# Latent attention with a gated feed-forward on one core: VectorE's remainder and low part between its two maxima, content copies in one write, numerators summed at other times

## What is computed

```python
xn  = layernorm(x)
q_c = ((xn @ Wq_down) @ Wq_up) as heads x 4;   q_r = (xn @ Wq_rope) as heads x 64
c_kv = xn @ Wkv_down;  k_c, v_c = c_kv @ Wk_up, c_kv @ Wv_up as heads x 4;  k_r = xn @ Wk_rope
a   = softmax((q_c . k_c + q_r . k_r) / sqrt(68))
s   = (a @ v_c) @ Wo
f   = lin(silu(lin(xn, w1q, a1, b1)) * lin(xn, w3q, a3, b3), w2q, a2, b2)
out = x + s * silu(f)          # lin(x, w, A, B) = x @ tile(w, 4).T + (x @ A.T @ B.T) / 2
```

## Time and profile before

| what | value |
|---|---|
| median of 3 runs | 2048.97 us (2047.34 to 2050.12) |
| profiled execution, its own time | 2049.55 us |
| its span, first to last instruction | 2046.7 us |
| mean granted TensorE clock | 0.986 of full speed |
| busy: PE, DVE, ACT, POOL | 92%, 71%, 68%, 69% of the span |
| chain that ended last: PE, DVE, DMA | 38%, 15%, 15% |

### The profile page before, as it was taken

How to read it: one execution, slowest core, us unless ns; L and a number is a source line. 1 busy time by engine, 2 the same in 40 slices (tenths; PEclk the granted TensorE clock), 3 DMA queues, 4 the chain that set the end, 5 groups by cost and what they waited for, 6 DMA issues and landing times.

```text
span 2046.7 us, 41685 instructions
## 1 busy us (share of the span) xinstructions
PE 1883.9 (92%) x12538; PEld 1479.3 (72%) x12538; DVE 1457.1 (71%) x1510; ACT 1386.3 (68%) x1884; POOL 1411.2 (69%) x1470
## 2 busy tenths in 40 slices
PE   9899999999999989998999999999999999887898
PEld 7777777777777767777777777777777777664666
DVE  8567777777776767677777777777767676565555
ACT  5557777777777777777777777777777776543222
POOL 5318787878778787878787878787877878104452
PEclk9999999999999999999999999999999999998999
DMA  8744444444444444444444444444444444555442
GB/s 262 205 92 109 92 107 91 104 96 99 102 100 91 94 104 91 108 93 110 90 106 91 105 96 99 102 100 104 93 99 90 108 92 99 138 125 162 146 134 72
DMA packets 186536, 225.23 MB, mean 110 GB/s; under 512 B 59710, under 2 KB 113758, under 8 KB 186462
## 3 DMA queue, kind: packets, MB, share of 16 engines
q1 hardware_dynamic: 186438, 224.57, 46.8%
q10 hardware_dynamic: 48, 0.03, 0.0%
HBM read 61.26 MB, written 35.65 MB: 47 GB/s over the span
## 4 chain that ended last, share of the span: by engine, by line
PE 38%; DVE 15%; DMA 15%; issue 13%; SPq 12%; POOL 2%; ACT 1%; DVEq 0%; ACTq 0%; POOLq 0%
PE st L1129 11%; DMA slot<-mrow 10%; PE pj L1163 8%; PE sx L1142 7%; DVE slot L1049 6%; PE ob L1095 6%; DVE mx L1041 6%; PE ob L1163 3%; SPq L740 2%; SPq L790 2%; DMA x_raw_h<-o_scratch 2%; SPq L736 2%; DVE kx L1035 1%; DVE pw L1063 1%; SPq L99 1%
## 5 line engine op out<-in xcount | busy, mean ns | idle before, releaser
L866 POOL TENSOR_TENSOR pw<-pf,pw 128x1024 f16<-128x1024 f32 x348 | 791.9, 2290 | 253.9 <-ACT pw L1022 214.0
L1041 DVE TENSOR_REDUCE mx<-sx 128x4 fp32r<-128x1024 f32 x512 | 627.1, 1225 | 450.0 <-PE sx L1142 445.2
L1129 PE MATMUL st<-slot,k 128*128 128x512 f32 x1024 | 418.2, 408 | 55.5 <-DMA slot<-mrow 47.0
L1013 ACT ACTIVATE pf<-st 128x1024 f32<-128x1024 f32 x464 | 446.5, 1011 | 33.0 <-PE st L1129 30.7
L1142 PEld LDWEIGHTS sx<-k,slot 88*128 88x128 f32 x2048 | 307.4, 191 | 165.6 <-DVE mx L1041 112.6
L1022 ACT ACTIVATE pw<-pf 128x1024 f16<-128x1024 f32 x348 | 355.2, 1055 | 93.0 <-PE ob L1095 82.3
L1142 PE MATMUL sx<-k,slot 88*128 88x256 f32 x2048 | 344.6, 291 | 75.5 <-DVE mx L1041 58.8
L1129 PE MATMUL st<-slot,krlh 128*128 128x512 f32 x1024 | 405.9, 396 | 0.0
L957 ACT ACTIVATE slot<-ob 64x512 fp32r<-64x512 f32 x256 | 151.6, 592 | 218.6 <-PE ob L1163 215.5
L1129 PEld LDWEIGHTS st<-slot,k 128*128 128x128 f32 x1024 | 194.3, 190 | 122.9 <-issue 82.6
L1129 PEld LDWEIGHTS st<-slot,krlh 128*128 128x128 f32 x1024 | 195.1, 191 | 36.3
(11 more groups left out here) (246 smaller groups left out, 2575.9 us busy)
## 6 DMA issues: line engine op xcount, KB each, us to landing
slot<-slot SPq DMA_DIRECT2D x256, 256.0 KB, 3.1
k<-kc SPq DMA_DIRECT2D x256, 128.0 KB
w_stage<-in_Wq_rope SPq DMA_DIRECT2D x64, 256.0 KB, 4.5
o_scratch<-o_sb SPq DMA_DIRECT2D x256, 64.0 KB
c_scratch<-stage SPq DMA_DIRECT2D x32, 256.0 KB, 3.1
c_in<-c_scratch SPq DMA_DIRECT2D x128, 64.0 KB, 2.2
k<-kc SPq DMA_DIRECT2D x128, 48.0 KB
k<-kx SPq DMA_DIRECT2D x128, 48.0 KB
```

What stands on the lines that cost most here:

```text
L866: nc.gpsimd.tensor_tensor(pw[:, s, kt, 1], pf[:, 2 * odd + kt], pw[:, s, kt, 0], ALU.subtract).then_inc(lo_done[kt][odd], 1)
L1013: nc.scalar.activation(dst, st[:, kt], ACT.Exp, scale=SCALE).then_inc(exp_done, 1)
L1041: nc.vector.tensor_reduce(mx[:, p, lo:lo + 4], sx[:, :, :].rearrange("p a (b k) -> p (a b) k", b=2), axis=AX.X, op=ALU.max).then_inc(red_d ...
L1129: last = nc.tensor.matmul(st[:, kt, h, :].rearrange("p (e n) -> p e n", e=PH), kk, q[:, s, :, h, :], start=(n == 0), stop=(n == 1))
```

## The change

1. **Content.** `content_hi` writes blocks 1 and 2 with one instruction (64 x 1024, `c_in` read twice), at s = 1 in place of s = 0. `content_lo` writes blocks 0 and 3 with one instruction (64 x 2 x 512), between the two maxima at s = 3 in place of behind both at s = 0. POOL's copies and their semaphore are gone. The blocks are now low, high, high, low, and the products that use them have the same sum.
2. **Remainder on DVE.** For one pair of steps of a turn it stands where it stood (it is now written at the start of the next step). For the other it moves from the end of an odd step to between the two maxima of the step behind it.
3. **PE.** In the two turns of the first group and of the last whose probabilities aren't split, `turn(k-8)` comes before `project(k)`.
4. **Finish.** Parts 0 to 5 of chunk 0 go to six tiles of their own and are loaded at k = 16 of the loop's last steps, parts 6 and 7 at k = 18. For the other chunks a pair of parts is loaded and added in each tile i, with the residual of that tile behind them, and the four `normalise` follow behind the loop over i. `output_hi` and `output_lo` of chunk c move from the `y` part of chunk c-1 into the tiles of chunk c itself: ACT at m = 8 and 9, DVE at m = 9 and 10. In DVE's step 18 a reciprocal comes earlier, and `b2` waits for all eight sums of chunk 0.

```diff
+def blocks_of(c):
+    return c[64:128, :].rearrange("p (i n) -> p i n", i=4)
+def twice(c_in):
+    return c_in[64:128, :].unsqueeze(1).broadcast_to([64, 2, CH])
...
-                        copies(k // NS + 1, at.turn(k) + 1)
-                        hold(pool, passed, ct_copy, 2 * at.turn(k) + 4)
...
-                nc.scalar.activation(content[parity % 2][:, 0, :], c_in[64:128, :], ACT.Copy).then_inc(ct_hi, 1)
+                nc.scalar.activation(content[parity % 2][:, 1:3, :], twice(c_in), ACT.Copy).then_inc(ct_hi, 1)
...
-                if s == (2 if at.first and k < NS else 0) and k < STEPS and at.live(k + NS):
+                if s == (2 if at.first and k < NS else 1) and k < STEPS and at.live(k + NS):
                     content_hi(k // NS + 1, at.turn(k) + 1)
...
-                nc.vector.tensor_tensor(c[:, 2, :], c_in[64:128, :], c[:, 0, :], ALU.subtract).then_inc(ct_lo, 1)
+                nc.vector.tensor_tensor(c[:, 0:4:3, :], twice(c_in), c[:, 1:3, :], ALU.subtract).then_inc(ct_lo, 1)
...
             def body(at, k):
+                split = k % 2 == 0 and at.live(k - 5) and at.split(k - 5)
+                if split and k % NS == 0:
+                    remainder(at, k - 5)
...
-                    for half in range(2):
-                        maxima(at, k - 1, half)
-                if k % NS == (2 if at.first and k < NS else 0) and k < STEPS and at.live(k + NS):
-                    content_lo(k // NS + 1, at.turn(k) + 1)
-                if k % 2 and at.live(k - 4) and at.split(k - 4):
-                    dve.wait_ge(hi_done[1][1], at.pairs(k - 4))
-                    nc.vector.tensor_tensor(pw[:, k % NS, 1, 1], pf[:, 3], pw[:, k % NS, 1, 0],
-                                            ALU.subtract).then_inc(lo_done[1][1], 1)
+                    maxima(at, k - 1, 0)
+                    if split and k % NS == 2:
+                        remainder(at, k - 5)
+                    if k % NS == 3 and k < STEPS and at.live(k + 1):
+                        content_lo(k // NS + 1, at.turn(k) + 1)
+                    maxima(at, k - 1, 1)
...
+                if k % NS == 0 and at.live(k - 2 * NS) and not at.split(k - 2 * NS):
+                    turn(at, k - 2 * NS)
                 project(at, k)
...
             load_num(sp, 0)
+            for n in range(KD + 2):
+                load_num_part(sp, 0, n)
...
+                if c + 1 < NC and i + 1 < NI:
+                    for n in range(2 * i + 2, 2 * i + 4):
+                        load_num_part(sp, c + 1, n)
...
-            if c + 1 < NC:
-                summed(c + 1)
             for i in range(NI):
                 if c + 1 < NC:
-                    normalise(c + 1, i)
+                    for n in (2 * i, 2 * i + 1):
+                        summed(c + 1, n)
...
+            if c + 1 < NC:
+                for kt in range(KD):
+                    normalise(c + 1, kt)
...
+                if m in (8, 9):
+                    for kt in (0, 1) if m == 8 else (2, 3):
+                        output_hi(c, kt)
...
+            dve.wait_ge(num_done, 2 * KD)
             nc.vector.scalar_tensor_tensor(out=blocks(b2), in0=blocks(hh[:, 0, :]), scalar=mk[:, 7:8], in1=b2_raw,
...
-                if starting(c) and m in (3, 4):
-                    for kt in (0, 1) if m == 3 else (2, 3):
-                        output_lo(0, kt)
+                if m in (9, 10):
+                    for kt in (0, 1) if m == 9 else (2, 3):
+                        output_lo(c, kt)
...
-                if c + 1 < NC:
-                    output_lo(c + 1, i)
```

More of the change, by code:

```diff
@@ L451, in scalar @@
                     act.wait_ge(c_loaded, 32)
-                    nc.scalar.activation(kc[64:128, 0:CH], c_in[64:128, :], ACT.Copy).then_inc(ct_hi, 1)
+                    nc.scalar.activation(blocks_of(kc)[:, 1:3, :], twice(c_in), ACT.Copy).then_inc(ct_hi, 1)
         def vector(dve):
@@ L548, in vector @@
                     dve.wait_ge(ct_hi, 1)
[L549 removed]
+                    nc.vector.tensor_tensor(blocks_of(kc)[:, 0:4:3, :], twice(c_in), blocks_of(kc)[:, 1:3, :],
                                             ALU.subtract).then_inc(ct_lo, 1)
@@ L646, in attention @@
         vt = sb(ctx, "vt", [128, 3, 4 * PH * NS * HD], BF16)
-        content = [c[64:128, :].rearrange("p (i n) -> p i n", i=4) for c in (kc, kx)]
+        content = [blocks_of(c) for c in (kc, kx)]
         krh = kc[0:64, :]
@@ L746, in content_split @@
             hold(sp, passed, ct_lo, at.turn(k) + 1)
-            hold(sp, passed, ct_copy, 2 * at.turn(k) + 2)
         def first_content(sp):
@@ L838, in body @@
                         pool.wait_ge(k1_filled, k + 3)
-                    if s == 2 and at.live(k + 2):
-                        if at.live(k - NS):
-                            hold(pool, passed, st_done, 2 * u - 6)
-                        if at.live(k - 5):
-                            if at.split(k - 5):
-                                hold(pool, passed, lo_done[0][1], at.pairs(k - 5))
-                            else:
-                                hold(pool, passed, vx_ready, u - 4)
-                        if k == 14 and not at.last:
-                            hold(pool, passed, w_ready, NS * at.g + NS + 1)
-                        copies(k // NS + 1, at.turn(k) + 1)
-                        hold(pool, passed, ct_copy, 2 * at.turn(k) + 4)
                 if at.live(k - 4) and k - 4 < STEPS:
@@ L907, in planes @@
                             ins.then_inc(vx_ready, 2)
-            def copies(parity, t):
-                c = content[parity % 2]
-                hold(pool, passed, ct_hi, t + 1)
-                for i in (1, 3):
-                    nc.gpsimd.tensor_copy(c[:, i, :], c[:, 0, :]).then_inc(ct_copy, 1)
             def refill(g, s):
@@ L1034, in content_lo, with remainder @@
                 dve.wait_ge(ct_hi, t + 1)
-                nc.vector.tensor_tensor(c[:, 2, :], c_in[64:128, :], c[:, 0, :], ALU.subtract).then_inc(ct_lo, 1)
+                nc.vector.tensor_tensor(c[:, 0:4:3, :], twice(c_in), c[:, 1:3, :], ALU.subtract).then_inc(ct_lo, 1)
+            def remainder(at, k):
+                dve.wait_ge(hi_done[1][1], at.pairs(k))
+                nc.vector.tensor_tensor(pw[:, k % NS, 1, 1], pf[:, 3], pw[:, k % NS, 1, 0],
+                                        ALU.subtract).then_inc(lo_done[1][1], 1)
             def maxima(at, k, half):
@@ L1157, in project @@
                 for c in range(KD):
-                    if c == 2 and k % NS == 0 and at.live(k - 2 * NS):
+                    if c == 2 and k % NS == 0 and at.live(k - 2 * NS) and at.split(k - 2 * NS):
                         turn(at, k - 2 * NS)
@@ L1304, in finish @@
     num_done = sem("num_done")
-    part_loaded = [sem(f"part_loaded{i}") for i in range(4)]
+    part_loaded = [sem(f"part_loaded{i}") for i in range(KD + 3)]
     xt_loaded = [sem(f"xt_loaded{i}") for i in range(2)]
@@ L1443, in sync_tail @@
             load_den(sp, 1)
+        if k == 18:
+            sp.wait_ge(num_done, KD)
             sp.wait_ge(r_stored, 16)
             spread_den(sp, 0)
-        if k == 18:
+            for n in range(KD + 2, 2 * KD):
+                load_num_part(sp, 0, n)
+        if k == 19:
             sp.wait_ge(recip, 2)
             store_recip(sp, 1)
-        if k == 19:
-            sp.wait_ge(at_sems.st_done, 2 * NS * NT)
-            for n in range(2 * KD):
-                load_num_part(sp, 0, n)
     def sync_rest(sp):
@@ L1469, in chunk @@
                 load_num(sp, c + 1)
-                for n in range(2 * KD):
+                for n in range(2):
                     load_num_part(sp, c + 1, n)
@@ L1514, in pool_rest, with summed @@
     def pool_rest(pool):
-        def summed(c):
-            pool.wait_ge(num_loaded, (c + 1) * 16 * KD)
-            for n in range(2 * KD):
-                if n >= KD:
-                    pool.wait_ge(num_done, c * 2 * KD + n - KD + 1)
-                pool.wait_ge(*parts_landed(c, n))
-                nc.gpsimd.tensor_tensor(num[:, n % KD, :], num[:, n % KD, :], num_part(c, n)[0],
-                                        ALU.add).then_inc(num_done, 1)
+        def summed(c, n):
+            tile, loaded, earlier = num_part(c, n)
+            if n == 0:
+                pool.wait_ge(num_loaded, (c + 1) * 16 * KD)
+            if n >= KD:
+                pool.wait_ge(num_done, c * 2 * KD + n - KD + 1)
+            pool.wait_ge(loaded, 16 * (earlier + 1))
+            nc.gpsimd.tensor_tensor(num[:, n % KD, :], num[:, n % KD, :], tile, ALU.add).then_inc(num_done, 1)
         def normalise(c, kt):
@@ L1540, in chunk @@
                 nc.gpsimd.tensor_tensor(res[:, i % 2, :], res[:, i % 2, :], xt[:, i % 2, :], ALU.add).then_inc(res_done, 1)
-        summed(0)
+            if c + 1 < NC:
+                for kt in range(KD):
+                    normalise(c + 1, kt)
+        for n in range(2 * KD):
+            summed(0, n)
         for kt in range(KD):
```

(6 more changed lines are left out.)

43 lines of the change are left out of this document (17 added, 26 removed).

## The result

The change made the kernel **0.55% faster**: ratio 0.9945, 95% interval 0.992 to 0.9969, medians 2035.93 us against 2048.16 us in the same comparison. That is 11 to 12 us, where the prediction had 27. The profiled execution of the changed kernel took 2040.67 us, span 2038.9 us, mean granted clock 0.980: it lies 4.7 us above its own median, so its span shows only 7.8 us of the gain. In that span the loop's first scores came 2.6 us later than in the profile before (96.14 in place of 93.52), the way from there to the first narrow product of chunk 0 got 24.4 us shorter (1759.2 to 1734.8), and the finish from there to PE's end 14.0 us longer (190.8 to 204.8).

A forecast was written before the change was run, and what follows sets the result against it. It took PE, busy 92% of the span, as the bound, with only its idle time to win. Loop −39 and finish +12 gave −27 from 2049.55: 2022.5 us, said as 2022, range 2000 to 2047.

The forecast's parts named there:

- What bounds the loop: Attention loop: PE's row scores wait for DVE's late maximum behind the low part; moving it wins 58.8 us at most.
- Steps 2 and 3: Loop: low part and remainder, 1.22 us each, move into DVE's holes of 1.31 and 0.84 us and cost nothing.
- the 0.8 us to spare: Loop: the late maximum can start 1.76 us earlier, PE needs 0.98 of it, leaving about 0.8 us.
- The rival of the lock: Loop: DVE between the maxima waits for POOL's instruction on the shared SBUF port, 1.5 us lost a turn: 2089 us, 8%.
- Step 5: Loop, refill turns: DVE's remainder delays the second maximum 0.48 us in three places, 1.4 us a change of group: +20 us.
- the 10 to 30 that I had named as a sign: Loop, 171 to 1731 us: PE's wait for the row of maxima rises by 10 to 30 us, in refill turns.
- The second rival: Loop: PE gives the 1.03 us a turn back at the wait for the row of maxima: loop 0, 2061 us, 5%.
- only its idle time can be won: Whole kernel: PE is busy 92% of the span, so the forecast counted only gains in its idle time.
- Steps 6 and 7: Finish: old waits go (21.2, 3.3, 2.25 us in chunks 0 to 2); a new wait for `ol` costs 8.75 us a chunk.
- I add 0.6: a wait of 6.4 us: Finish, every chunk: PE's first `attn_out` waits 5.8 us for `ol`, plus 0.6 for ACT's roundings ahead of a gate.
- Step 8: Chunk 0 and loop end: `b2` waiting for all eight sums costs +2.5 us; six more loads cost +1, between 0 and 3.
- loop −21 to −48 with the finish at +2 to +19: The prediction's own case for the whole kernel, given 64% and stated as 2003 to 2043 us.

The follow-up runs named there:

- experiment 3: Loop-only kernel with the low part, in its new two-block form, and ScalarE's write back at s = 0 behind both maxima: 2094.53 us, ratio 1.022.
- experiment 4: Loop-only kernel with two of a turn's four output stores moved on SyncE from ahead of the odd row of maxima to behind it: 1994.28 us, ratio 0.9728.
- experiment 9: Changed kernel with the parts of chunks 1 to 3 loaded and added ahead of the tiles i, as before the change: 2047.56 us, ratio 1.0003.
- Loop-only: The changed attention loop with the finish of the kernel before: 2015.15 us, ratio 0.982 to the kernel before.
- finish-only: The loop of the kernel before with the changed finish: 2064.36 us, ratio 1.0087 to the kernel before.

## Why the prediction was right and wrong

- **What bounds the loop (right).** The stall at the row scores came from the low part's place; it went with the move, and came back, larger, with the low part (experiment 3). It was 0.98 us in three of a group's four turns; in the first, 0.81. The whole loop was worth 33 to 37 us where the sum had 39, but that agreement is in part luck, as the fourth point shows.
- **Steps 2 and 3, the holes (right in effect, wrong in the low part's duration).** I took 1.22 us for both. In ordinary turns the moved remainder took 1.22 to 1.25 us, the low part some 1.6, since POOL was at work beside it. In the refill turns they took up to 2.9 and 2.3 us. In the ordinary turns the 0.8 us to spare covered it, as I had it; PE had no wait there for the maxima. The rival of the lock, 2089, didn't come about: the remainder of 3.02 us ended 1.08 us after POOL's instruction of 2.15 us that ran from 1031.74, and never did DVE wait for two. In 171 to 1731 us of the changed kernel 144 of 173 remainders and low parts of DVE took over 1.3 us; every one of them ended 1.08 to 1.09 us behind the end of one POOL instruction. The Trainium skill, "SBUF — State Buffer", section "SBUF: two separate sides", has the blocked engine wait for the other's whole instruction; these rows agree.
- **Step 5, the refill turns (two places of three right, the size small).** I had 0.48 us in three places of a group, 1.4 us, all at the transposes and their row. Means over 14 groups: 0.54 and 0.67 at the transposes, and 1.07 before the values' products, 2.3 us. The third is not what I had: it comes from the remainder that stayed in front of the queries and takes 3.02 us there.
- **What the sum of the loop left out.** In ordinary turns the wait for the row of maxima rose from 0.3 to 0.8 us, which the sum had at nothing. Over the window it rose by 17 us, inside the 10 to 30 that I had named as a sign, but hardly in the turns with a refill, which I had named: of the two waits there one fell from 1.45 to 1.15 and one rose from 1.42 to 1.88. The second rival named this wait and its chance was small because it was small before; it came in part. Its cause wasn't in the sum: the row lands 4.5 us after its issue in the mean of such turns, 4.1 before, behind two stores (experiment 4). Set against it, a turn without the stall gets shorter by more than the stall: the step that had 0.98 us of it went from 6.92 to 5.68 us. The sum counted idle time alone ("only its idle time can be won"): 39 us, some 2.5 a group. The idle time fell by 0.7 a group, 11 us over 16 groups, which is under the 21 that I gave as the least; PE's busy time fell by 1.4 a group besides. I didn't foresee that, and its reason is open.
- **Steps 6 and 7, the finish (the mechanism right, the size wrong).** Chunk 0 was forecast at −10 and came to −11; chunks 1 to 3 at +5.5, +6.5 and +8.75 and came to +7.0, +7.3 and +10.8. The step that failed is "I add 0.6: a wait of 6.4 us": it took the numerators as there in time; only the bound allowed for late ones. 6.42 us is what chunk 0 waits, and every chunk in experiment 9; in chunks 1 to 3 of the change the parts are late and it is 8.25 to 9.31. The slow products behind it, which I had at 2.35 us, were about right: the 24 products of a chunk's first two outputs took 8.31, 7.57, 7.51 and 7.29 us where they took 5.62 without a wait. PE had been idle for 6.42 to 9.31 us; over the first twelve products the mean granted clock was 0.50 to 0.63 (0.50 is the level of 1.2 GHz, 1.00 that of 2.4), and over the 24 without a wait 1.00.
- **Step 8 (the b2 term right, the loads too small).** For `b2` I had +2.5; the waits for `hid` at 1835.20 and 1839.92 come to 2.26. For the loads at the loop's end I had +1 us. The last row of maxima landed 7.1 us after its issue where it took 4.92, at 1820.30, and PE waited 3.92 us for it in place of 1.75 (the row above says "issue", but PE went on 0.09 us behind the landing). The eight score products behind that took 3.75 us at a granted clock of 0.50, in place of 2.06 at 1.00: +4 in all. Loop-only, without these loads, already has a landing of 5.5, a wait of 2.33 and 3.26 us of products, so beside it they cost +2; in finish-only, beside the kernel before, +4. My bound was 3.
- **The sum.** −39 and +12 stood for what came, alone, as −33 to −37 and +16 to +18. Each lies inside the ends that I gave it; both missed toward slower, and a difference of two such terms takes the whole of both errors: −18 to −19 in place of −27. The change itself came to −11 to −12; the last 7 us are within the intervals, and no run says what they are. So the mechanisms came, and what failed are sizes: the wait of 6.4 us in chunks 1 to 3 (8.25 to 9.31), the loads (+2 to +4 for +1), and in the loop the refill turns (2.3 us a group for 1.4) and the row's wait in ordinary turns, put at nothing (0.5 us more). One slip is in the chances: loop −21 to −48 with the finish at +2 to +19 ends at 2048, not at 2043.

## What to carry to other kernels

A wait that is removed is worth what the next limit of the same turn lets through: here the row of maxima, whose landing hung on two stores queued just ahead of it, and then the place of the values' products. Look for what is queued ahead of a small transfer that an engine waits for, and move the loads and writes that nobody waits for behind it; and check who waits for what stands behind them now, for the same move cost 84 us in the kernel before. In a pipelined stage, follow the chain that one tile's buffer closes (free, load, sum, use) and compare its length with the stage's own period before its steps are moved apart.

## What the runs showed that I had not expected

- Two stores of 64 KB ahead of an 8 KB row cost its landing 2.3 to 2.7 us (4.1 and 4.5 against 1.8, in the mean of ordinary turns), while a 256 KB copy ahead of it cost none that can be seen.
- The time of one kernel spreads as much here as the change gained: 2030.67 to 2046.12 us for the changed kernel in eight runs, 2042.71 to 2055.47 for the kernel before. The start of the loop came at 93.5, 94.2 and 96.1 us in the three profiles with the old loop, and between 94.6 and 98.5 in the eleven with the new one. Ahead of it the change touches only the first turn's content. Whether that costs the 2 us between the means, no run shows.
